# Deep stage of a 12-sublayer kernel: one norm power per tile, a step later; short products split in halves; new order on four engines

## The reference

```python
def attn_layer(x, Wqkv, qs, ksc, Wo):              # 16 heads of 64, windows of 32
    q, k, v = split(x @ Wqkv)
    q = l2norm(q) * qs ; k = l2norm(k) * ksc       # norm over the 64 of a head
    q, k = rotary(q), rotary(k)
    out = local_attention(q, k, v)                 # 32 queries x 64 keys, softmax
    return out @ Wo
def ffn_layer(x, g, bln, W1, b1, W2, b2):
    xn = (x - mean) / sqrt(var + 1e-5) * g + bln
    a, gate = split(xn @ W1 + b1)                  # 341 each
    return a * gelu(gate) @ W2 + b2
for i in range(6):
    x = attn_layer(shift_tokens(x), ...) + x
    x = ffn_layer(shift_tokens(x), ...) + x
```

## Time and profile before

| | |
|---|---|
| time, median of 3 runs (lowest to highest) | 5142.4 us (5136.1 to 5149.9) |
| span of the profiled execution | 5148.7 us |
| PE busy | 4508.2 us, 88% |
| DVE busy | 3456.9 us, 67% |
| POOL busy | 3075.1 us, 60% |
| ACT busy | 2317.0 us, 45% |

### The profile page before, as it was taken

How to read it: one execution, slowest core, us unless ns; L and a number is a source line. 1 busy time by engine, 2 the same in 40 slices (tenths; PEclk the granted TensorE clock), 3 DMA queues, 4 the chain that set the end, 5 groups by cost and what they waited for, 6 DMA issues and landing times.

```text
span 5148.7 us, 147111 instructions
## 1 busy us (share of the span) xinstructions
PE 4508.2 (88%) x66028; PEld 2555.2 (50%) x66028; DVE 3456.9 (67%) x4153; ACT 2317.0 (45%) x2523; POOL 3075.1 (60%) x1713
## 2 busy tenths in 40 slices
PE   6898689977468999999999999568999999999998
PEld 3444333333135555555555555235555555555554
DVE  4365536632437778778777776447877787888885
ACT  1242134433134555555555555234555555555553
POOL 0010000000019889888889997049988899998984
PEclk7699679976569999999999999669999999999999
DMA  2000000000001112111111111101111111112111
GB/s 71 1 1 1 0 0 1 1 0 0 0 22 32 30 29 55 29 51 32 52 29 53 31 29 33 44 9 29 33 51 30 35 49 30 54 29 55 30 32 29
DMA packets 78094, 144.43 MB, mean 28 GB/s; under 512 B 18728, under 2 KB 24944, under 8 KB 75824
## 3 DMA queue, kind: packets, MB, share of 16 engines
q1 hardware_dynamic: 77488, 135.23, 10.1%
HBM read 39.75 MB, written 1.05 MB: 8 GB/s over the span
## 4 chain that ended last, share of the span: by engine, by line
PE 47%; issue 23%; POOL 21%; DVE 7%; ACT 1%; DMA 0%; SPq 0%; DVEq 0%; POOLq 0%
POOL arena L1446 8%; PE psum L1033 8%; POOL arena L1439 6%; POOL arena L1452 5%; PE psum L1050 4%; PE psum L1064 4%; PE psum L1102 4%; PE psum L1083 4%; PE psum L1002 3%; PE psum L1148 3%; PE psum L1097 2%; PE psum L1142 2%; PE psum L524 2%; POOL rstd L1457 2%; PE psum L1016 2%
## 5 line engine op out<-in xcount | busy, mean ns | idle before, releaser
L1446 POOL TENSOR_TENSOR arena<-arena,minus_half 128x16 f32<-128x16 f32 x384 | 1131.9, 2948 | 32.0
L1439 POOL TENSOR_TENSOR arena<-arena 128x1024 f32<-128x1024 f32 x384 | 909.8, 2369 | 13.5 <-DVE arena L1324 13.5
L1452 POOL TENSOR_TENSOR arena<-arena 128x1024 f32<-128x1024 f32 x384 | 733.7, 1911 | 42.6
L1320 DVE TENSOR_TENSOR arena<-psum,arena 128x1024 f32<-128x1024 f32 x384 | 468.1, 1219 | 404.1 <-ACT arena L1202 404.1
L1462 POOL MEMSET arena<- 128x33 f32 x4 | 0.4, 128 | 995.3 <-DVE std L1686 995.3
L1208 ACT ACTIVATE arena<-psum 128x1024 f32<-128x1024 f32 x384 | 392.2, 1021 | 298.8 <-PE psum L1050 298.4
L1202 ACT ACTIVATE arena<-psum 128x1024 f32<-128x1024 f32 x384 | 392.3, 1022 | 246.5 <-PE psum L1033 243.4
L1324 DVE TENSOR_TENSOR arena<-psum,arena 128x1024 f32<-128x1024 f32 x384 | 466.8, 1215 | 54.1 <-PE psum L1050 54.1
L1050 PEld LDWEIGHTS psum<-w_ident,arena 128*128 128x128 f32 x3072 | 355.3, 141 | 281.9 <-issue 148.5
L1331 DVE TENSOR_REDUCE arena<-arena 128x16 f32<-128x1024 f32 x384 | 464.8, 1211 | 2.8
L1235 ACT ACTIVATE arena<-psum 128x1024 f32<-128x1024 f32 x192 | 196.7, 1024 | 580.7 <-PE psum L1064 580.7
(11 more groups left out here) (260 smaller groups left out, 7703.9 us busy)
## 6 DMA issues: line engine op xcount, KB each, us to landing
arena<-arena SPq DMA_DIRECT2D x672, 128.0 KB, 2.3
deep_wqkv<-in_deep_wqkv SPq DMA_DIRECT2D x6, 1536.0 KB, 7.1
arena<-in_deep_wqkv SPq DMA_DIRECT2D x6, 1536.0 KB, 7.2
arena<-arena SPq DMA_DIRECT2D x96, 64.0 KB, 2.5
deep_wo<-in_deep_wo SPq DMA_DIRECT2D x6, 512.0 KB, 7.5
arena<-in_deep_wo SPq DMA_DIRECT2D x6, 512.0 KB, 7.4
deep_w<-in_deep_w SPq DMA_DIRECT2D x6, 341.0 KB, 7.6
arena<-in_deep_w SPq DMA_DIRECT2D x6, 341.0 KB, 7.5
```

What stands on the lines that cost most here:

```text
L1320: nc.vector.tensor_tensor(turned[:, hs, :].rearrange("p h (a e) -> p h a e", a=2), swapped, sin, ALU.mult).then_inc(de.deep_rope_parts, 1)
L1439: nc.gpsimd.tensor_tensor(roped[:, hs, :], roped[:, hs, :], turned[:, hs, :], ALU.add).then_inc(de.deep_summed, 1)
L1446: nc.gpsimd.tensor_tensor(h_inv[a % 2][:, hs], h_inv[a % 2][:, hs], minus_half[:, :], ALU.pow).then_inc(de.deep_inv_ready, 1)
L1452: nc.gpsimd.tensor_tensor(roped[:, hs, :], roped[:, hs, :], over(h_inv[a % 2][:, hs], [P, LHEADS, LD]), ALU.mult).then_inc(de.deep_roped, 1)
```

## The change

Five things change in the deep stage, nothing outside it.

1. The norms' clamp and power are one instruction each per tile, over 32 columns (16 heads of Q and 16 of K), where they were two each over 16. They and both scalings now stand a step later on POOL: step s runs them for tile s-1, and then adds the parts of tile s.
2. `roped` has two buffers by tile; `h_sum` has one; `qT` is two buffers of one tile.
3. `scores_pe` and `mix_pe` are cut in halves of 32 products. Between the score halves stands `value_pe`; between the mix halves stand the K turn and, by step, a gate or mean product.
4. PE's order: scores and values come right behind the Q product, the unit's products and the K product after them, and only then the Q turn.
5. ACT takes `exp_act` after the K square and the Q turn's copy. DVE takes the K parts before the row sums, but at t = 3 after the division.

```diff
-        def mix_pe(pe, c, j):
+        def mix_open_pe(pe, c, j):
...
+            mix_pe(j, 0)
+        def mix_close_pe(pe, c, j):
+            mix_pe(j, 1).then_inc(de.deep_pv_done, 1)
...
                 if s < ALL:
                     qk_pe(pe, c, s, 0)
+                if 0 <= s - 2 < ALL:
+                    scores_open_pe(pe, c, s - 2)
+                    value_pe(pe, c, s - 2)
+                    scores_close_pe(pe, c, s - 2)
...
+                if t == 3 and begun:
+                    wo_rest_pe(pe, c, n - 1)
+                if s < ALL:
+                    qk_pe(pe, c, s, 1)
                 if 0 <= s - 1 < ALL:
                     turn_pe(pe, c, s - 1, 0)
+                if 0 <= s - 3 < ALL:
+                    mix_open_pe(pe, c, s - 3)
...
                 if s < ALL:
                     square_act(act, c, s, 1)
+                if 0 <= s - 1 < ALL:
+                    turn_act(act, c, s - 1, 0)
+                if 0 <= s - 2 < ALL:
+                    exp_act(act, c, s - 2)
...
+                if t == 3 and begun:
+                    attn_dve(dve, c, n - 1)
+                if s < ALL and t != 3:
+                    parts_dve(dve, c, s, 1)
                 if 0 <= s - 2 < ALL:
                     row_sum_dve(dve, c, s - 2)
                     divide_dve(dve, c, s - 2)
+                if s < ALL and t == 3:
+                    parts_dve(dve, c, s, 1)
...
+        def norms_pool(pool, c, a):
+            i = c * ALL + a
+            pool.wait_ge(de.deep_sq_summed, 2 * i + 2)
+            nc.gpsimd.tensor_scalar(h_inv[a % 2], h_sum, NORM_FLOOR, None, ALU.max).then_inc(de.deep_clamped, 1)
+            pool.wait_ge(de.deep_clamped, i + 1)
+            nc.gpsimd.tensor_tensor(h_inv[a % 2], h_inv[a % 2], minus_half[:, :], ALU.pow).then_inc(de.deep_inv_ready, 1)
...
-                if s < ALL:
-                    rope_sum_pool(pool, c, s, 0)
+                if 0 <= s - 1 < ALL:
+                    norms_pool(pool, c, s - 1)
+                    rope_scale_pool(pool, c, s - 1, 0)
+                    rope_scale_pool(pool, c, s - 1, 1)
                 if t == 0 and 0 <= n - 2 < UNITS:
                     rstd_pool(pool, c, n - 2)
                 if s < ALL:
-                    rope_inv_pool(pool, c, s, 0)
-                    rope_scale_pool(pool, c, s, 0)
-                    rope_inv_pool(pool, c, s, 1)
+                    rope_sum_pool(pool, c, s, 0)
                     rope_sum_pool(pool, c, s, 1)
-                    rope_scale_pool(pool, c, s, 1)
```

More of the change, by code:

```diff
@@ L946, in program @@
         tabs = new(4, TILES, LD)
-        qT = new(PAIRS, T)
+        qT = [new(PAIRS, P) for _ in range(2)]
         kT = new(PAIRS, WIN + T)
@@ L951, in program @@
         turned = new(2 * LHEADS, LD)
-        roped = new(2 * LHEADS, LD)
+        roped = [new(2 * LHEADS, LD) for _ in range(2)]
         probs = [new(PAIRS, 2, 2 * WIN) for _ in range(2)]
@@ L957, in program @@
         xs = [new(WIN + T) for _ in range(2)]
-        h_sum, h_inv = [new(2 * LHEADS) for _ in range(2)], [new(2 * LHEADS) for _ in range(2)]
+        h_sum, h_inv = new(2 * LHEADS), [new(2 * LHEADS) for _ in range(2)]
         row_max, row_sum, row_inv = (new(LHEADS) for _ in range(3))
@@ L997, in scores_pe, with scores_close_pe @@
                                      stop=False, skip_group_check=True)
-            for pair in range(PAIRS):
+            scores_pe(j, 0)
+        def scores_close_pe(pe, c, j):
+            scores_pe(j, 1).then_inc(de.deep_scores_ready, 1)
+        def scores_pe(j, part):
+            t = j % TILES
+            for pair in range(PAIRS // 2 * part, PAIRS // 2 * (part + 1)):
                 for jj in range(WPT):
@@ L1039, in turn_pe @@
             pe.wait_ge(de.deep_roped, 2 * i + half + 1)
[L1040 removed]
+            if half == 1:
+                pe.wait_ge(de.deep_turn_kept, 2 * i + 1)
+            elif a >= 1:
                 pe.wait_ge(de.deep_v_kept, i)
[L1042 to L1047, removed]
             for m in range(PAIRS):
                 h = LHEADS * half + 2 * m
[L1050 removed]
+                last = nc.tensor.matmul(turns[:, m * P:(m + 1) * P], roped[a % 2][:, h:h + 2, :], w.ident[:, :], start=True, stop=True,
                                         is_transpose=True)
@@ L1075, in mix_pe @@
             apart(pe)
-            for pair in range(0, PAIRS, 2):
+            mix_pe(j, 0)
+        def mix_close_pe(pe, c, j):
+            mix_pe(j, 1).then_inc(de.deep_pv_done, 1)
+        def mix_pe(j, part):
+            t = j % TILES
+            for pair in range(PAIRS // 2 * part, PAIRS // 2 * (part + 1), 2):
                 for jj in range(WPT):
```

91 lines of the change are left out of this document (33 added, 58 removed).

## The result

| | before | after |
|---|---|---|
| time, median (lowest to highest) | 5141.0 us (5136.1 to 5149.9) | 5393.6 us (5384.1 to 5397.0) |
| span of the profiled execution | 5148.7 us | 5389.3 us |

The change makes the kernel slower: ratio 1.0487, 95% interval 1.0468 to 1.0506. The forecast was 5361, in a range from 5205 to 5450.

The account below looks back on a forecast made before the run. Neither PE (66 us per cycle) nor POOL (62) alone bounded the 69.95 us cycle, but how they are hooked together. The new cycle, 74.5, adds 4.55 over 48 cycles: +218, 5367 profiled, 5361 as median; range 5205 to 5450.

Parts of the forecast that it names:

- The price of the power: POOL's power over 32 columns: 5.5 us, on the line of both measured widths, against 5.86 for two of 16.
- The walk: One four-step cycle summed from POOL's K scaling at t = 2: 74.9 us, taken as 74.5, against 69.95 before.
- Steps 1 and 2: PE from the K turn at +1.3 through 20.7 us of work in one piece; the Q turn stands at 22.0.
- Step 3: ACT copies the Q turn and only then takes the exponential, though its input was ready earlier; now at 24.1.
- Step 4: DVE at t = 3: row sum, reciprocal and division 2.68 us, then K parts 2.37; done at 29.2.
- Step 5: POOL adds K only now, after about nine us idle; sum, clamp, power and scalings 12.1, tile scaled at 41.3.
- step 6: POOL's next two tiles at 14.5 us each, `rstd_pool` 1.0, and the division's lock against POOL's sums: 33.6 us.
- what would show it: Trace signs listed beforehand, among them PE's idle before the turns, ended by POOL, growing from 48 to well over 150 us.
- The halves: Cut scores and mix remove PE's 98.8 us of stops, 2.1 per cycle, for about 0.1 per step; counts only where PE sets the cycle.
- the trace disagrees: Claim against the skill's mostly hidden instruction fetch: 65.2 us of stops in PE's runs of 256 instructions.
- PE sets the cycle: Rival: POOL loosened so PE never waits, halves remove stops; 66.5 us per cycle, 4977 us; chance 0.11.
- Cheap power: Rival: POOL's power costs mostly per instruction, 2.93 to 4.3 us over 32 columns; cycle 72, about 5245 us; chance 0.18.

Follow-up runs that it names:

- Experiment 2: Changed kernel, but at t = 3 ACT takes the exponential ahead of the K square and the Q turn's copy; 5248.8 us, ratio 1.0210.
- experiment 1: Changed kernel, but DVE takes the K parts ahead of the row sum at t = 3 too; 5356.9 us, ratio 1.0409.
- 9: Changed kernel with, at t = 3, both the exponential ahead of the K square and the K parts ahead of the row sum; 5359.2 us, ratio 1.0417.
- experiment 7: Changed kernel with POOL's power over Q's 16 columns alone, K's left out; 5348.4 us, ratio 1.0400.
- kernel 12: kernel 5 with DVE's two shift copies moved to the end of the step t = 1; 5092.1 us, ratio 0.9893 to the kernel before.
- experiment 3: Changed kernel with scores and mix in one run each, values ahead of the scores, mix behind the K turn; 5478.3 us, ratio 1.0643.
- 6: Kernel before with both scores and mix cut in halves, all else as before; 5268.1 us, ratio 1.0235.
- kernel 4: Kernel before with one power per tile a step later and the second buffers, old order and whole runs; 6687.5 us, ratio 1.3000.
- kernel 5: Changed kernel's operations, halves and late norms included, in another order of all four engines; 5183.1 us, ratio 1.0068 to the kernel before.

## Why the prediction was right, point by point

**The price of the power.** Forecast 5.5, measured 5.457 (median of 192, 5.455 at least): both lower widths and this one lie on one line. Right.

**The walk.** 0 is 2371.26 in the timelines above, the end of L1465. Steps 1 and 2: the Q turn done at 22.0; measured 21.9. Step 3: exponential done at 24.1; 24.0. Step 4: K parts done at 29.2; 29.0. Step 5: the tile scaled at 41.3; 41.8 in this cycle, with 0.64 us of `tabs_pool` (L1446) that the walk left out and that not every cycle has (the K sum's idle before is 9.51, "about nine"). Over 40 cycles, by the ends of the K scalings (L1465), the way to this point takes 41.3 us in the mean and the rest, step 6 with its 33.6, takes 33.5. The cycle came out at 74.9, the sum before I took 0.4 off it for hand-offs that would overlap. No such overlap shows, and the 0.4 are 19 of the 22 us between forecast and profile (5367 against 5389). Experiment 2 shows that step 3 matters: the exponential's place is worth 145 us.

**Where the walk was too simple.** It treats the late K sum as the one thing to cure. Experiments 1 and 9 cured it and gained 37 and 34 us, since a second chain of nearly the same length runs beside it: K parts, division, turned probabilities, Q product. Its length is 74.1 to 74.2: that is the cycle of kernels 1, 9 and 7, and in 1 and 7 POOL has 2% and 1% of the chain that ended last. So the measured time alone says little for the walk: three powers shorter by 2.5 us each took only 0.7 off the cycle (experiment 7). What speaks for the walk is that its marks agree one by one. The prediction named neither PE's waits for the division (101.5 us in the whole execution) nor what PE's waits do to its clock. Nor did the turns' idle time pass 150: it is 139.6, of which 111.5 by POOL. This sign in "what would show it" was wrong.

**The halves.** The stops are gone, as forecast. Their price is not "about 0.1 per step", 0.4 per cycle: the short matmuls' busy time rises by 31.5 and 40.6 us, 1.5 per cycle, of the 2.1 that the stops cost. Part of that is the lower clock; in kernel 12, at a granted clock of 1.00, it is 60.5 us, 1.3 per cycle. So where PE sets the cycle, 38 us of the stops' 98.8 are left as a gain, as an estimate from these rows. In the changed order the halves are worth 85 us (experiment 3), for the greater part, by its trace, because the first half of the mix fills the time between the turns; in the order of before they cost 122 (6). Their sign is set by who waits for the pieces, not by the stops. The sum held them at nothing, and that holds only roughly: without the halves the cycle is 77.2.

The Trainium skill, "Runtime: NRT & Kernel Launch", section "Instruction fetch mechanics", says that crossing into the next block is mostly hidden. No run here shows that the stops are fetches at all; the profile only names no semaphore for them. In whole runs they add up to 98.8 us before, but to 32.4 in kernel 3 and to 8.3 in kernel 4, where PE waits much elsewhere. With halves it is nothing in the changed kernel and 6.1 us in kernel 12. So the prediction's "the trace disagrees" says more than the rows show.

**The rivals.** PE sets the cycle: it did not in the changed kernel, but does in kernel 12, at 68.7, where the rival had 66.5. Of the 2.2, 0.9 are the halves' busy time beyond my 0.4 (326.6 and 439.1 us in that kernel, 60.5 above before: 1.3 per cycle), 0.8 the idle rest, and some 0.5 I can't assign. Cheap power: the power was not cheap. Had it been, the time would have been 5348 rather than the 5245 worked out (experiment 7): the chain beside POOL's takes 74.2 per cycle, where this rival put it at 72. The second buffers "cost nothing": they gain 19 us, so this holds to within 0.4%.

**The lock.** Step 6 took the division as the one DVE operation that meets POOL. Its median went from 1.226 to 1.432 us, while the maximum stayed near (3.401 before, 3.193 after). So it is held more often than the one time per cycle that I set, though step 6 came out as summed all the same:

```profile
L1321 DVE TENSOR_TENSOR arena<-arena x192: 1224/1432/3193, 1557.3 to 5339.5; 128x1024 f32<-128x1024 f32 x192
```

Experiments 5 and 12 show that copies within SBUF are longer beside POOL's work as well. The line of the second copy in kernel 5:

```profile
L1515 DVE COPY arena<-z 64x511 f32<-64x511 f32 x45 | 90.2, 2005 | 1.4
```

and in kernel 12:

```profile
L1515 DVE COPY arena<-z 64x511 f32<-64x511 f32 x45 | 20.0, 443 | 1.4
```

2.0 us against 0.44 each. The first of the two copies (L1514) did not gain: 1.3 us in kernel 5 and 1.6 in kernel 12, in the mean of the same 45. The Trainium skill, "SBUF — State Buffer", section "Who interferes with whom", has the port pair that DVE and GpSimd share as an exclusive lock; these rows agree.

What stays open: how much of the 253 us each place of the change's order costs by itself. Only the places named in experiments 1, 2, 5 and 12 were moved apart; the way from 5249 (kernel 2) to 5183 (kernel 5) is the other order as a whole.

## What to carry to other kernels

When a stage goes back and forth between engines, walk one cycle with the lists of all engines beside each other and look where an instruction that is ready stands behind one that is not: one exponential placed behind a square and a copy cost 145 us. After a cure, walk again, since a second chain of nearly equal length may lie beside the first (experiments 1 and 9). And judge a change of operations apart from the order that came with it: the same operations took 5394 us in one order and 5092 in another.

## What was not expected of the hardware

After some idle times of about two microseconds, PE ran at half its rate for a while. The changed kernel, PE in two places, then the row of `--windows` for what followed the second (the granted clock is the third number from the end):

```profile
2335.68 1.09 PE L1054 MATMUL psum<-w_ident,arena 128*128 128x128 f32 x8 [1.77 <-POOL arena L1465]
2336.71 1.83 PE L1093 MATMUL psum<-arena 64*64 64x32 f32 x64
2338.47 1.96 PE L1054 MATMUL psum<-w_ident,arena 128*128 128x128 f32 x8
...
2411.21 1.28 PE L1054 MATMUL psum<-w_ident,arena 128*128 128x128 f32 x8 [2.36 <-POOL arena L1465]
...
2412.40:2421.60 9.20, 9.20 (x153) 8.72 (x153) 4.61 (x5) 4.74 (x5) 9.12 (x6) 0.50 0.01 4
```

1.83 and 1.96 us, where 1.14 and 1.04 are the rule: the lower of the two levels, 1.2 GHz, instead of 2.4. Behind the 2.36 us it lasted over nine microseconds. Not every such wait does this: the 1.69 us in experiment 1 (2412.01) were followed by a turn of 1.09. Over 1750 to 3150 us the granted clock is 1.00 before, 0.98 after and in kernels 1 and 9, 0.95 in kernel 3, 0.86 in kernel 4, 1.00 in kernels 2 and 12. So a wait of PE can cost more than its length: in experiment 1 the idle 1.91 us at 2394.02 were followed by 1.8 us lost in the two operations behind it.
